# Attention softmax: maxima and sums by strided reductions on VectorE, other softmax work on two tiles an instruction

## What is computed

```python
def _L0_xattn_ref(latents, context, Wq, Wk, Wv, Wo, q_norm_w, k_norm_w):
    kv = jnp.concatenate([context, latents], axis=1)      # 1601 + 256 = 1857 rows
    q = (latents @ Wq)...                                 # 32 heads of 128
    k = (kv @ Wk)...; v = (kv @ Wv)...                    # 8 kv heads
    q = rms_norm(q, q_norm_w); k = rms_norm(k, k_norm_w)
    scores = einsum('bhgqd,bhkd->bhgqk', qg, k) / sqrt(128)
    probs = softmax(scores, axis=-1)
    out = einsum('bhgqk,bhkd->bhgqd', probs, v)
    return out @ Wo
x = x + tanh(g_xattn) * _L0_xattn_ref(_layernorm(x), ctx_4096, ...)
x = x + tanh(g_ffn) * _L0_ffn_ref(_layernorm(x), ...)
```

## Time and profile before

| | |
|---|---|
| Median of 3 runs | 3668.18 us (3655.16 to 3674.81) |
| Span of the profiled execution | 3683.3 us |
| TensorE busy (matmul) | 3184.8 us, 86% |
| VectorE busy | 3152.2 us, 86% |
| ScalarE busy | 2121.6 us, 58% |
| GpSimd busy | 1668.6 us, 45% |

### The profile page before, as it was taken

How to read it: one execution, slowest core, us unless ns; L and a number is a source line. 1 busy time by engine, 2 the same in 40 slices (tenths; PEclk the granted TensorE clock), 3 DMA queues, 4 the chain that set the end, 5 groups by cost and what they waited for, 6 DMA issues and landing times. The chain is left out here.

```text
span 3683.3 us, 52901 instructions
## 1 busy us (share of the span) xinstructions
PE 3184.8 (86%) x14138; PEld 2429.3 (66%) x14138; DVE 3152.2 (86%) x3890; ACT 2121.6 (58%) x3795; POOL 1668.6 (45%) x1175
## 2 busy tenths in 40 slices
PE   7978898889798988887989889878888888599699
PEld 5856666666476666665766666656666666277477
DVE  6856999999979999999799999988999999732666
ACT  3435666666656666666666666666666666431211
POOL 2322556555536555555455555544555555400000
PEclk9989999999999999999999999999999999799799
DMA  7870000000200000011000100110100000153400
GB/s 239 263 230 24 29 28 28 28 28 29 73 33 29 28 28 31 35 46 48 33 29 31 44 30 28 35 57 27 42 32 29 28 28 12 54 172 97 150 34 18
DMA packets 179314, 210.99 MB, mean 57 GB/s; under 512 B 10452, under 2 KB 125140, under 8 KB 174056
## 3 DMA queue, kind: packets, MB, share of 16 engines
q1 hardware_dynamic: 174408, 196.27, 16.2%
q0 software_dynamic: 2176, 8.39, 0.7%
q10 hardware_dynamic: 2592, 4.72, 0.4%
HBM read 140.14 MB, written 69.21 MB: 57 GB/s over the span
## 5 line engine op out<-in xcount | busy, mean ns | idle before, releaser
L855 POOL TENSOR_TENSOR att_sm<-att_sm,att_sc 128x512 f32<-128x512 f32 (+1 forms) x832 | 1305.6, 1569 | 545.9 <-ACT att_sc L732 490.1
L656 PE MATMUL att_ppv<-att_pr,att_V 128*128 128x512 f32 (+1 forms) x2880 | 907.6, 425 | 191.5 <-DVE att_pr L802 185.0
L732 ACT ACTIVATE att_sc<-att_sc 128x512 f32<-128x512 f32 (+1 forms) x960 | 611.9, 637 | 642.5 <-DVE att_sc L798 642.1
L802 DVE TENSOR_TENSOR att_pr<-att_sc,att_pr 128x512 fp32r<-128x512 f32 (+1 forms) x960 | 924.0, 964 | 0.7 <-ACT att_pr L736 0.7
L787 DVE TENSOR_TENSOR att_mx<-att_mx,att_sc 128x512 f32<-128x512 f32 (+1 forms) x832 | 883.6, 1062 | 41.2 <-ACT att_sc L729 38.5
L635 PE MATMUL att_pqk<-att_q,att_kT 128*128 128x512 f32 (+1 forms) x2880 | 881.3, 415 | 3.1 <-DVE att_kT L824 2.3
L605 PE MATMUL att_pkv<-att_ctxT,att_wkv 128*128 128x512 f32 (+1 forms) x3072 | 799.3, 384 | 75.9 <-DVE att_kT L824 71.8
L656 PEld LDWEIGHTS att_ppv<-att_pr,att_V 128*128 128x128 f32 (+1 forms) x2880 | 529.6, 198 | 421.4 <-DVE att_pr L802 318.0
L729 ACT ACTIVATE att_sc<-att_pqk,att_rk 128x512 f32<-128x512 f32 (+1 forms) x960 | 656.2, 684 | 129.1 <-PE att_pqk L635 123.8
L605 PEld LDWEIGHTS att_pkv<-att_ctxT,att_wkv 128*128 128x128 f32 x3072 | 564.0, 192 | 218.7 <-DVE att_kT L824 98.6
L736 ACT CAST att_pr<-att_sc 128x512 fp32r<-128x512 f32 (+1 forms) x960 | 599.3, 624 | 176.2 <-PE att_ppv L656 172.2
(11 more groups left out here) (129 smaller groups left out, 2697.2 us busy)
## 6 DMA issues: line engine op xcount, KB each, us to landing
q_scr<-pre_qT SPq DMA_DIRECT2D x128, 256.0 KB, 3.5
att_wkv<-kv_scr SPq DMA_DIRECT2D x32, 1024.0 KB, 4.8
...
```

Of the source, the lines that this page charges most:

```text
L656: mm = pe.matmul(ppv[:], V[0:m, vp, t], pr[0:m, pp, (h * NT + t) % NP], start=(t == 0 and i == 0), stop=(t == NT - 1 and i == 2))
L732: act.activation(sc[0:m, s], sc[0:m, s], ACT.Exp).then_inc(exp_ok, 1)
L802: dve.tensor_tensor(pr[0:m, LO, s % NP], sc[0:m, s], pr[0:m, HI, s % NP].bitcast(F32), ALU.subtract).then_inc(plo_ok, 1)
L855: pool.tensor_tensor(sm[0:m, h], sm[0:m, h], sc[0:m, s], ALU.add).then_inc(sum_ok, 1)
```

## The change

**Maxima.** The 14 running maxima of a half become three `tensor_reduce` over tiles 0 to 5, 6 to 11 and 12 to 14 (`MAXG`). Each reads the score buffer as `[p, n, t]`: for each of 512 columns it steps through the tiles, 2 KiB apart. `sc` gets 17 places a half in place of 15: places 6 and 13 take the partial results, and the next reduction begins with them, so the three read 6, 7 and 4 places. The partitions of the last tile beyond its 65 rows are set once to -3.0e38. `mx` is gone; the result goes to place 6.

**Sums.** They move from GpSimd to VectorE: three `tensor_reduce` of 6, 7 and 3 places and one `tensor_tensor` of 65 rows for the last tile, into a single `sm`. GpSimd keeps `pow` alone.

**Two tiles an instruction.** `exp`, `hi` and `lo` go over two tiles, as `sub` did (`GR`, 8 groups a half). `pr` has NP = 2 places of two tiles.

**Order and loads.** `LAG` goes from 21.5 to 24, and the places of the softmax steps are rewritten. `vraw` shrinks from 15 tiles to two chunks, so `vhi` of a chunk waits for `vt` two chunks before, and the places of `v` go from 1, 4, 6.63, 11.35 to 1, 6, 13, 17.5, and those of `vt` from 10.6, 15.5, 20.25, 24.37 to 12.6, 16.6, 20.6, 24.6. The weights of a round are loaded in two DMAs, for k and for v. The loads of the next context come later (places 28.1, 28.1, 34.1 and 37.1 in place of 22.1, 25.1, 28.1 and 32.1).

```diff
-    NP = 3
+    NP = 2
     NR = NC + 1
+    GR = [(t, min(t + 2, NT)) for t in range(0, NT, 2)]
+    MAXG = ((0, 6), (6, 12), (12, NT))
+    SLOTS = NT + 2
+    MAXIMUM = 6
+    def slot(t):
+        return t + (t >= MAXG[1][0]) + (t >= MAXG[2][0])
...
-        LAG = 21.5
+        LAG = 24
+            for g, (t, z) in enumerate(GR):
+                p = h * NT + t + LAG
+                steps += [(p - 4.3, "sub", h, g), (p - 3.2, "exp", h, g), (p - 2.4, "hi", h, g), (p - 1.6, "lo", h, g)]
+            for i, (t, z) in enumerate(MAXG):
+                steps += [(h * NT + z - 1 + 1.1, "max", h, i), (h * NT + z - 2 + LAG - 1.5, "sum", h, i)]
...
-        for c, (k, v, vt) in enumerate(((-12.7, 1, 10.6), (-9, 4, 15.5), (-3.21, 6.63, 20.25), (-1.5, 11.35, 24.37))):
+        for c, (k, v, vt) in enumerate(((-12.7, 1, 12.6), (-9, 6, 16.6), (-3.21, 13, 20.6), (-1.5, 17.5, 24.6))):
...
                     elif what == "max":
-                        dve.wait_ge(sc_ok, AHEAD + T + 1)
...
-                            dve.tensor_tensor(mx[0:m, h], mx[0:m, h], sc[0:m, s], ALU.max).then_inc(max_ok, 1)
+                        a, z = MAXG[t]
+                        i, k = slot(a) - (t > 0), slot(z - 1) + 1
+                        dve.wait_ge(sc_ok, AHEAD + tiles(n, h, z - 1))
+                        dve.tensor_reduce(sc[:, h, k if t < len(MAXG) - 1 else MAXIMUM], sc[:, h, i:k].rearrange("p t n -> p n t"),
+                                          AX.X, ALU.max).then_inc(max_ok, 1)
...
-                        dve.wait_ge(phi_ok, AHEAD + T + 1)
-                        dve.tensor_tensor(pr[0:m, LO, s % NP], sc[0:m, s], pr[0:m, HI, s % NP].bitcast(F32),
-                                          ALU.subtract).then_inc(plo_ok, 1)
+                        dve.wait_ge(phi_ok, AHEAD + grouped(n, h, t))
+                        dve.tensor_tensor(pr[0:m, LO, t % NP, 0:w], sc[0:m, h, i:i + w], pr[0:m, HI, t % NP, 0:w].bitcast(F32),
+                                          ALU.subtract).then_inc(plo_ok, w)
+                    elif what == "sum":
+                        a, z = MAXG[t]
+                        i = slot(a) - (t > 0)
+                        dve.wait_ge(exp_ok, AHEAD + tiles(n, h, z - 1))
...
+                            dve.tensor_reduce(sc[:, h, k], sc[:, h, i:k].rearrange("p t n -> p n t"),
+                                              AX.X, ALU.add).then_inc(sum_ok, z - a)
...
-                    if what == "sum":
-                        pool.wait_ge(exp_ok, AHEAD + T + 1)
...
-                            pool.tensor_tensor(sm[0:m, h], sm[0:m, h], sc[0:m, s], ALU.add).then_inc(sum_ok, 1)
...
-                        act.wait_ge(vt_ps, AHEAD + NC * (n - 1) + t + 1)
+                        act.wait_ge(vt_ps, AHEAD + NC * n + t - 1)
```

134 lines of the change are left out of this document (71 added, 63 removed).

## The result

| | before | after |
|---|---|---|
| Median | 3671.5 us (4 runs) | 5005.2 us (4 runs) |
| Ratio, with its 95% interval | | 1.363 (1.359 to 1.367) |
| Span of the profiled execution | 3683.3 us | 5011.0 us |

The prediction was 3877 us with a range of 3700 to 4750. The kernel got slower, as forecast, but by 1334 us and not by 209, and the time lies above the range. It is also above the 4875 us at the upper end of the rival of strided elements.

A forecast was written before the change was run, and what follows sets the result against it. The prediction took VectorE to set the pace, with about 84 us of work in a round of 88.3. 3683 + 131 + 64 + 14 = 3892 us, less 15 us to the median: 3877 us, range 3700 to 4750.

The forecast's parts named there:

- rival of strided elements: VectorE's reductions pay up to 0.92 ns more per strided element, 31 us a round: 4875 us at the upper end; chance 0.32.
- GpSimd's hold-up: VectorE's low parts, maxima and `dred` diagonals run faster once GpSimd's sums go: -19.7 us a round.
- VectorE's work without a stride price: With sums, maxima and low parts changed, VectorE's work stays at 84 us a round to within 1 us; the sum used 83.2.
- the 4625 us beside the page's price: Estimated time if reductions paid the Trainium skill's 1.73 ns a column, 23 us more a round.
- I take 1.04 ns: Price per element of VectorE's strided reductions, taken equal to contiguous ones; 1.96 ns kept for the range.
- The walk: Hand walk through the order of steps: VectorE idles 9.2 us a round, round 92.4 us, +4.1 us a round, +131 us.
- the bank wait: Second half: TensorE's `v` of chunk 3 waits for `vtlo` of chunk 1 behind a reduction, 6.0 us; VectorE then idles 2.8 us.
- The other half has no such bank wait: In the other half VectorE idles only 0.5 us at a `klo` and 1.8 us at a low part behind `oraw`.
- the ring at `mb`: No term of the prediction: `mb` on TensorE waits for the last `sub`, behind a 7-place reduction; VectorE idles 4.79 and 1.70 us.
- the pair of reductions in a row: Reductions of 6 and 7 places, 7.1 us once a half: TensorE stands 5.2 us, which costs VectorE little.
- TensorE's clock: Stalls bring TensorE more time at 1.2 GHz: 2 us a round, between nothing and 6, +64 us.
- The ends: Ends of batch elements: `LAG` is 2.5 places longer, four drains cost between nothing and 29 us, taken as +14 us.

The follow-up runs named there:

- n1_no_sums: The kernel before with GpSimd's running sums on one column in place of 512, so the sums are left out: 3196.8 us, ratio 0.870.
- c1_contig: The changed kernel with its reductions over 3 to 7 tiles reading the same block contiguously (wrong groups, only the time is of use): 4263.7 us, ratio 1.160.
- m2_hops: The kernel before plus a block timing single VectorE instructions at steps of 32 bytes to 2 KiB; `tensor_tensor` with one hopping source: 1.80 ns a column, contiguous 1.12.
- m1_micro: The kernel before plus a block timing single VectorE reductions, strided and contiguous; strided over four or more places in SBUF: 1.72 to 1.77 ns an element.
- c4_contig_sum: c1_contig with `vt` of chunk 1 moved to 15.6 and the second sum reduction moved behind the last tile's `sub`: 3964.2 us.
- w1_wide_pairs: The kernel before with sums on VectorE, maxima and sums as `tensor_tensor` over two neighbouring tiles with a fold at the end: 3541.0 us, ratio 0.964.

## Why the prediction was wrong, step by step

- **GpSimd's hold-up, -19.7 us a round:** right, 19.3 (n1_no_sums). **VectorE's work without a stride price:** the parts listed add up to nothing (-19.7 + 18.9 + 1.7 - 0.9), which leaves the 83.8 to 84.0 us of before, and 83.82 were measured (c1_contig). The 83.2 in the sum has no such source; the 0.6 to 0.8 us are 19 to 26 us of the time. In the same way the 4625 us beside the page's price count from the profiled execution, where 3877 counts from the median; from there it is 4613.
- **"I take 1.04 ns":** wrong, and the first of the two large errors. It is 1.72 to 1.77 ns in SBUF from four places on. The term was 0, it measured 21.8 us a round, 699 us. This is the strided rival, to which I gave 0.32, with up to 31 us a round, and 23 by the price of the page. The choice went by the nearest rows in kind, contiguous reductions of a single place, which say nothing of a step. The argument that a reduction has the lighter traffic didn't hold either: it pays as much an element as the `tensor_tensor` of m2_hops pays a column. The Trainium skill, "Vector Engine (DVE) Microarchitecture Reference", section 5.2, has 1.73 ns for a two-source operation with one hopping source; L189 of m2_hops, with its fixed cost, is near it with 1.80 ns. Its sentence that a one-source operation between two regions runs at full rate isn't contradicted (in m1_micro a reduction of 2 places takes 1.23 us strided and 1.22 contiguous), but it doesn't carry to four places, and I let it weigh for the forecast. The same section gives as a rule that a port has its full rate only with runs of two or more adjacent words. The reductions here over four to eight places in SBUF, whose steps leave no such runs, pay 1.72 ns an element and more, as that rule has it; those over three places pay little and those over two nothing.
- **The walk, 9.2 us of idle VectorE a round:** wrong as it stands, 21.9 in c1_contig and 24.05 in the change. The failed step is the sentence on what is queued behind the bank wait: "`pv` of tiles 8 and 9, `mb` and the rest". The walk treated `mb` as work and didn't ask what `mb` itself waits for, in either half. `mb` waits for a `sub` behind the same reduction, and `hi` stands on ScalarE behind a `copy` whose `qk` stands behind `mb`. So the walk had VectorE idle 2.8 us where it is 6.3. The larger miss is the other half, of which the prediction says "The other half has no such bank wait": the ring at `mb` has 6.5 us there (4.79 + 1.70 in c1_contig) that the walk hasn't at all. With both rings away, the round takes 95.3 us (c4_contig_sum), where the forecast has 92.4 and 2 for the clock. That this is so near is partly luck. The bank wait and its 2.8 us are gone there too; the walk's other terms, 2.3, 1.8, 0.5 and 1.8 us, measured 1.98, 1.77, 0.70 and 1.47; and 5.0 us of idle VectorE stand in no term of it (3.16 before `var`, 1.25 before `dred`, 0.58 before `red`). On the pair of reductions in a row the walk was right (TensorE waits 3.1 us there in c1_contig, not 5.2, and it costs nothing more).
- **The bank wait, called the main new cost:** it is there (5.5 us in c1_contig, 7.8 in the change, forecast 6.0), but taking it away alone gives nothing, since the wait of `mb` behind it takes over.
- **TensorE's clock, +2 us a round:** the clock does fall behind the waits, and what that costs lies inside the idle time above; no run separates it, so the 2 us stay unmeasured. The granted clock is 0.89 in a round of c1_contig, 0.93 in one of c4_contig_sum and 0.80 in the change, 1.00 in w1_wide_pairs. I expected under 0.94.
- **The ends, +14 us:** in c4_contig_sum the spans differ by 280.8 us and 32 rounds of 7.0 us make 224, so 57 us are left for the ends and whatever in the measured round isn't typical. In the change 32 rounds already make up all but 3 us. What the ends cost stays open.
- **Signs.** Low parts of 1.22 us, a clock under 0.94, and VectorE waiting for `hi` behind that `vtlo` came. TensorE's waits came longer than the 5 to 6 us: 7.8 before the `v` matmul released by `vtlo`, and 7.8 and 7.4 before `pv` behind the double reductions. A round of 92 to 95 us didn't come. The wait for `pmax` went from 58 to 12 us. Reductions at 3.35 us didn't; the prediction named 4.8 us and more as the sign of the rival, and that is what came.
- **The range:** it ended at 4750 since it took the stride's price and the walk's idle time as two separate risks. Both fell out badly: 21.8 us a round for the stride lie inside the rival's 31, but with the waits of the forecast they would have made some 4575 us. VectorE's idle time in the change is 2.2 us a round over that of c1_contig, and its time 741 us over it, not 699.
